# Two graph-attention layers: smaller gather batches, and a wait for a later tile's adjacency before each

## What is computed

```python
h = jnp.maximum(_layernorm(x, axis=-1), 0.0)
x = x + _L0_gnn_ref(h, adj, L0_gnn_W, L0_gnn_a)     # e = leaky_relu(s1_i + s2_j); softmax over adj > 0; elu(att @ hW)
h = jnp.maximum(_layernorm(x, axis=-1), 0.0)
x = x + _L1_gnn_ref(h, adj, Wq, bq, Wk, bk, Wv, bv) # e = q_i . k_j / sqrt(128);  softmax over adj > 0; elu(att @ v)
```

## Time and profile before

| | |
|---|---|
| median of 3 runs | 1950.41 us (1947.33 to 1957.92) |
| the profiled execution, its own time | 1946.39 us |
| its span, first to last instruction | 1944.6 us |
| start-up, first table of rows, first masks | to about 134 us, when the first gather goes out |
| first phase at its regular pace | about 152 to 925 us |
| its end without adjacency traffic | 925 to 1034 us |
| second phase | about 1056 to 1930 us |

### The profile page before, as it was taken

The page is one execution under the profiler, slowest core; times in us unless marked ns, Lnnn a source line. Parts: engine busy times, 40 slices in busy tenths (PEclk is TensorE's granted clock), DMA queues, the critical chain, the costliest instruction groups (busy, mean ns, idle before and its releaser), DMA issues.

```text
span 1944.6 us, 23228 instructions
## 1 busy us (share of the span) xinstructions
PE 1202.7 (62%) x5362; PEld 932.8 (48%) x5362; DVE 1290.0 (66%) x6912; ACT 766.3 (39%) x1507; POOL 1135.2 (58%) x1206
## 2 busy tenths in 40 slices
PE   2666767766677767766533456666565656556566
PEld 1444544443454445444433355555555555555555
DVE  4476888867898869877853455556565655556565
ACT  1966666656677758765111011111111111111111
POOL 1236666665666666665654566666666666666662
PEclk9887777777777777777555566666666666666665
DMA  9979999997999989995221112222222222222121
GB/s 307 408 283 398 389 367 350 359 330 274 368 393 388 326 315 387 384 370 180 56 53 45 44 49 55 53 54 54 49 55 53 55 54 55 54 54 54 48 56 35
DMA packets 122263, 372.41 MB, mean 192 GB/s; under 512 B 34577, under 2 KB 67858, under 8 KB 89362
## 3 DMA queue, kind: packets, MB, share of 16 engines
q1 hardware_dynamic: 75458, 289.83, 39.2%
q0 software_dynamic: 38464, 81.08, 15.5%
q10 hardware_dynamic: 8208, 0.03, 0.3%
HBM read 358.12 MB, written 12.72 MB: 191 GB/s over the span
## 4 chain that ended last, share of the span: by engine, by line
DVE 42%; another core or an unknown queue 21%; PE 13%; issue 9%; DMA 8%; ACT 3%; POOL 3%; SPq 1%; DVEq 0%; ACTq 0%; POOLq 0%
DVE arena L884 10%; DMA arena<-table,arena 6%; PE psum L1403 5%; DVE arena L1133 5%; POOL arena L580 3%; ACT arena L1184 2%; PE psum L1363 2%; DVE arena L877 2%; DMA table<-arena 2%; DVE arena L1137 2%; DVE arena L709 2%; DVE arena L902 2%; PE psum L1428 1%; DVE arena L768 1%
## 5 line engine op out<-in xcount | busy, mean ns | idle before, releaser
L580 POOL DMA_INDIRECT arena<-table,arena x576 | 555.8, 965 | 339.3 <-issue 204.7
L612 POOL DMA_INDIRECT arena<-table,arena x576 | 551.0, 957 | 327.2 <-DVE arena L893 159.5
L1184 ACT ACTIVATE arena<-arena 128x2048 bf16<-128x2048 int32 x256 | 485.7, 1898 | 58.0 <-remote 32.1
L1410 PE MATMUL psum<-arena 128*128 128x131 f32 (+1 forms) x768 | 193.1, 417 | 326.3 <-DVE arena L877 242.8
L1410 PEld LDWEIGHTS psum<-arena 128*128 128x128 f32 x768 | 160.4, 302 | 339.5 <-issue 336.4
L1363 PE MATMUL psum<-arena 128*128 128x512 bf16 x1024 | 309.4, 458 | 12.6 <-ACT arena L1184 12.6
L884 DVE SCALAR_TENSOR_TENSOR arena<-arena 128x131 f32<-128x131 f32 (+1 forms) x768 | 272.1, 354 | 18.8 <-DVE arena L884 2.2
L865 DVE TENSOR_TENSOR arena<-psum,arena 128x18 f32<-128x18 f32 x128 | 22.2, 174 | 326.9 <-remote 323.7
L1403 PE MATMUL psum<-arena 128*128 128x1 f32 x768 | 147.4, 307 | 148.0 <-DVE arena L867 137.3
L1403 PEld LDWEIGHTS psum<-arena 128*128 128x128 f32 x768 | 147.2, 273 | 181.3 <-DVE arena L867 158.5
L1320 ACT ACTIVATE arena<-psum 128x384 f32<-128x384 f32 x64 | 31.5, 492 | 425.8 <-remote 334.5
(11 more groups left out here) (199 smaller groups left out, 2112.9 us busy)
## 6 DMA issues: line engine op xcount, KB each, us to landing
arena<-in_adj_dram SPq DMA_DIRECT2D x256, 1024.0 KB
arena<-table,arena POOLq DMA_INDIRECT x1152
table<-arena POOLq DMA_DIRECT2D x32, 132.0 KB, 6.1
arena<-table SPq DMA_DIRECT2D x64, 66.0 KB
table<-arena SPq DMA_DIRECT2D x16, 256.0 KB
arena<-table SPq DMA_DIRECT2D x64, 64.0 KB
out_dram<-arena SPq DMA_DIRECT2D x16, 256.0 KB
arena<-in_x_dram SPq DMA_DIRECT2D x4, 0.5 KB, 12.2
```

The source lines that it names most:

```text
L580: pool.indirect_dma_start(Gt[:, v % GROUP, c + 1, :], None, table0, bass.IndirectOffsetOnAxis(idx_now[:, v % GROUP, c:c + 1], 0))\
L612: pool.indirect_dma_start(Gt[:, t % GROUP, c + 1, 0:D], None, table1, bass.IndirectOffsetOnAxis(idx_now[:, t % GROUP, c:c + 1], 0))\
L1184: nc.scalar.activation(mask[:, k, q * QUARTER:(q + 1) * QUARTER], adj_sb[:, k, q, :], ACT.Relu, accum_out=sum_all[:, bass.ds(tile, 1), q:q ...
L1410: last = nc.tensor.matmul(acc_ps[k][:, 0:width], weighted[:, c, :], Gt[:, r, OWN + c, 0:width], start=(c == 0), stop=(c == CHUNKS - 1))
```

## The change

The nine gathers of a tile are cut in four batches, of 3, 2, 2 and 2, in both phases. `landed` still asks for batch n-2, which now leaves at most five on the way (4, when both batches have two). In the first phase POOL waits in addition, ahead of batch b of tile v, for `mask_done` to reach 4(v+7)+b: for b = 0 that tile v+6 is masked entirely, for b = 1, 2, 3 that the first, the first two, the first three quarters of tile v+7 are masked. DVE waits for four semaphores of rows where it waited for three. The branch that isn't executed uses four semaphores of the second phase in place of its own `w_adj_used`.

```diff
@@ -34,8 +34,10 @@
 QCOLS = CHUNKS * 128
 GROUP = 4
 
-BATCH = 3
-BATCHES = 3
+FIRST = (0, 3, 5, 7, 9)
+BATCHES = 4
+SIZE = [FIRST[n + 1] - FIRST[n] for n in range(BATCHES)]
+BATCH_OF = [n for n in range(BATCHES) for _ in range(SIZE[n])]
 QUARTERS = 4
 WIDTH = 132
 LISTED = 129
@@ -366,7 +368,8 @@
         w_h_turned = sem("w_h_turned")
         w_ht_done = sem("w_ht_done")
         w_adj_in = [sem(f"w_adj_in{q}") for q in range(QUARTERS)]
-        w_adj_used = [sem(f"w_adj_used{q}") for q in range(QUARTERS)]
+
+        w_adj_used = [h_col_done, h_col_sb, u_done, u_kept]
         w_u_done = sem("w_u_done")
         w_ut_done = sem("w_ut_done")
         w_cbias_done = sem("w_cbias_done")
@@ -568,18 +571,21 @@
 
                 if n >= 0:
                     tile, nth = n // BATCHES, n % BATCHES
-                    pool.wait_ge(rows_in[tile % GROUP][nth], 16 * BATCH * (tile // GROUP + 1))
+                    pool.wait_ge(rows_in[tile % GROUP][nth], 16 * SIZE[nth] * (tile // GROUP + 1))
 
             for v in range(T):
                 if v >= GROUP:
                     pool.wait_ge(summed, v - 3)
                 pool.wait_ge(idx_done, v + 1)
                 for c in range(ROWS - 1):
-                    if c % BATCH == 0:
-                        landed(BATCHES * v + c // BATCH - 2)
+                    if c in FIRST:
+                        landed(BATCHES * v + BATCH_OF[c] - 2)
+
+                        if v + 7 < T:
+                            pool.wait_ge(mask_done, QUARTERS * (v + 7) + BATCH_OF[c])
                     pool.indirect_dma_start(Gt[:, v % GROUP, c + 1, :], None, table0,
                                             bass.IndirectOffsetOnAxis(idx_now[:, v % GROUP, c:c + 1], 0))\
-                        .then_inc(rows_in[v % GROUP][c // BATCH], 16)
+                        .then_inc(rows_in[v % GROUP][BATCH_OF[c]], 16)
 
             pool.wait_ge(flag_done, 1)
             whole = pool.value_load(flag[0:1, 0:1], min_val=0, max_val=1)
@@ -607,11 +613,11 @@
                     pool.wait_ge(summed, T + t - 3)
                     pool.wait_ge(idx_done, T + t + 1)
                     for c in range(ROWS - 1):
-                        if c % BATCH == 0:
-                            landed(BATCHES * (T + t) + c // BATCH - 2)
+                        if c in FIRST:
+                            landed(BATCHES * (T + t) + BATCH_OF[c] - 2)
                         pool.indirect_dma_start(Gt[:, t % GROUP, c + 1, 0:D], None, table1,
                                                 bass.IndirectOffsetOnAxis(idx_now[:, t % GROUP, c:c + 1], 0))\
-                            .then_inc(rows_in[t % GROUP][c // BATCH], 16)
+                            .then_inc(rows_in[t % GROUP][BATCH_OF[c]], 16)
 
 
         @block.vector
@@ -851,7 +857,7 @@
 
             def score0(u, k, r, n):
                 for batch in range(BATCHES):
-                    dve.wait_ge(rows_in[r][batch], 16 * BATCH * n)
+                    dve.wait_ge(rows_in[r][batch], 16 * SIZE[batch] * n)
                 dve.wait_ge(self_in[r], 16 * n)
                 nc.vector.tensor_tensor(e10[:, :], Gt[:, r, :, D], s1_10[:, r, :], ALU.add).then_inc(e_done, 1)
                 dve.wait_ge(e_done, u + 1)
@@ -1127,7 +1133,7 @@
 
                 def score1(u, b, k, n):
                     for batch in range(BATCHES):
-                        dve.wait_ge(rows_in[b][batch], 16 * BATCH * n)
+                        dve.wait_ge(rows_in[b][batch], 16 * SIZE[batch] * n)
                     dve.wait_ge(self_in[b], 16 * n)
                     for c in range(OWN):
                         nc.vector.scalar_tensor_tensor(out=prod[:, c, :], in0=Gt[:, b, c, 0:DE], scalar=SCALE, in1=u_row[:, b, P:],
```

## The result

The changed kernel takes 2055.41 us, the median of 4 runs (2045.34 to 2060.84), against 1951.41 us for the kernel before in the same measurement (4 runs, 1947.33 to 1957.92): a ratio of 1.0522, with a 95% interval of 1.0489 to 1.0556. It is 104 us slower; the forecast was 2035 us, 84 us slower. The profiled execution took 2054.3 us, its span is 2052.4 us, 107.8 us more than before.

What follows compares the result with a forecast made beforehand. First phase bound by transfers, its gather chain setting the pace up to 412 us; second phase not. 1946.4 + 85 (first phase; other terms 0) = 2031 us profiled, plus 4.0 to the median: 2035 us, range 1940 to 2085.

Steps and rivals of the forecast that it cites:

- The law of the chain: First phase, POOL's gathers: a tile costs 1.5L + 3.75 before, 2L + 3.75 after; 15.6 us a tile, +85 us.
- L: Time from the start of a batch's last gather to the start it releases; 6.65 us before by the law.
- The prediction's formula: First phase: L = 3.5 + 2.9 x 13.1/P for a tile of P us, giving P = 15.6.
- The unloaded end: L with DMA engines unloaded: taken as 3.5 us, between 2.9 and about 5.0.
- the loaded value: L with DMA engines loaded: taken as 6.4 us, range 6.2 to 6.65.
- the 6.54 us of tile 23's first batch: First phase after a 10 us pause: return time cited against the "faster" rival (L mostly queueing among gathers; 0.17, about 1922 us).
- The head start and the stall: First phase: the slower chain loses POOL's head start, swallows the 15.9 us ACT stall and stays late through tile 55.
- The mask wait at nothing: POOL's mask wait, first phase: free, as adjacency leads when gathers are late, and otherwise `score0` comes at least 13.8 us on.
- DVE's fourth wait at nothing: DVE's extra semaphore wait, ahead of L856 and L1133: under 2 us in each phase, taken as 0.
- bounds 0 and +10, taken as 0: Second phase: no wait if L is 3.5; at L of 5.0, 13.75 us of POOL against a 13.6 us period.
- The end of the first phase: 925 to 1034 us, without adjacency: POOL can send at 11.3 us a tile against 13.6 each; taken as 0.
- The rule weighed: Skill's DMA rule, about 2.0 us plus bytes: L an estimated 3.1, chain 10.0 us a tile, the change costing nothing.

Runs made afterwards that it cites:

- e1: Changed kernel without the mask wait (batches of 3, 2, 2, 2 in both phases): 2047.99 us, ratio 1.0472 to the kernel before.
- e5: Five batches of 2, 2, 2, 2 and 1, no mask wait: 2117.79 us, with 1989.43 for the kernel before on that chip.
- e13: Kernel before, its second phase pausing POOL ahead of the seventh gather until tile t-2's scatter matmuls are done; another chip: 1769.18 us, ratio 1.0001.
- e8: Batches of 3, 2, 2, 2 without mask wait, plus unused adjacency loads in the second phase: 2201.69 us, against 1952.28 before.
- e7: Kernel before (batches of three) plus unused adjacency loads, four quarters a tile, in the second phase: 1985.48 us, against 1952.28 before.
- e2: Kernel before, batches of three, plus only the mask wait: 1954.99 us, ratio 0.9996.
- e10: Kernel before with six of nine gathers a tile in the second phase, result incomplete: 1733.65 us, against 1952.28 before.
- e6: Changed kernel with each batch waiting for the landing of batch n-3 instead of n-2, both phases: 2007.18 us, ratio 1.0272.
- e12: Batches of 5 and 4 without mask wait (as another run), plus a POOL pause in each phase: 2003.91 us, ratio 1.0075 to the kernel before.

## Why the prediction was right

**The law of the chain held in the first phase.** Batches 0 and 2 of a tile form one chain, and it costs 2L + 3.75. Predicted 15.6 us a tile and 858 us for 55, measured 15.59 and 857.5. e1 has it without the mask, e5 with five batches, and e13 for three batches without any other limit. That the pace gives back a plausible L is no test by itself, since the distances on a chain add up to the pace whether POOL waits or not; the test is that POOL stood still before batch 2 in 54 of 56 tiles and before batch 0 in 41 of 55, and that `score0` waited behind them. One L for every batch was too simple: in e8 the other chain decides.

**L fell as it was made to.** The prediction's formula gives 3.5 + 2.9 x 13.1/15.6 = 5.94 us, and the measured pace 5.92. The unloaded end was a little low: in the new second phase, where adjacency is gone, released batches stand 3.8 to 4.3 us behind, not 3.5. With 4.0 in its place the formula would have said 15.7 us a tile. The DMA share came to 0.87 for 0.84. Only the reason for the loaded value had been argued; e7 shows it, by adding adjacency and nothing else. The argument itself had a hole: the 6.54 us of tile 23's first batch were not free of other gathers, for the three of the second batch went out while it was under way, between 456.84 and 463.38.

**The head start and the stall.** That the slower chain would swallow the single stall and stay late to tile 55 was right: `score0` waits 38 times, to the end. "Nearly every tile" was too much: it is 38 of 56, with 4.2 us a time (2 and more was said), and in the rest the rows were there first. POOL's landing waits number 109, or about 137 with those named after the mask but owed to landings, and I had said over 150: batches 1 and 3, on the chain with 1.25 us to spare, often find their landing there.

**The mask wait at nothing:** e2, 0.9996 (0.9959 to 1.0032). The prediction had two reasons, and both turned out to be needed: in the changed kernel the masks are ahead, and in e2, where they are not from tile 19 on, the wait is still free, since `score0` needs a batch only in a later iteration.

**DVE's fourth wait at nothing:** nothing in the profiles speaks against it; it was not tried by itself.

**What failed was the second phase, "bounds 0 and +10, taken as 0".** It measured +15.5 (+10 in e1). The working asked only whether POOL has the time, and L of 3.8 to 4.3 against a distance of 3.75 is a delay of a few tenths. I had not seen that the phase's period is tied to the end of POOL's run through DVE's wait (e10), so that there is no slack to take up a disturbance: in the pairs DVE meets a second wait of 4 us. What sets a pair off is open. The row that shows this wait, 303.4 us of 800, was in the trace of before and I had read only POOL's side of it. The end of the first phase, also 0, measured +4.7, and the start +3.0, neither of them traced to the change. These three and the smaller distance between profile and median (1.1 us here, 4.0 before) are the whole difference between 2035 and 2055.

**The rule weighed** ("DMA: Bandwidth & Descriptors", Anatomy of one DMA, SWDGE path, of the Trainium skill, about 2 us plus the bytes) would have had the change free. Under load no run comes near its estimate of 3.1 us: the released batches of after, e7 and e8 stand 5.6 to 8.3 us behind (medians by batch). The same page's section on latency expects a slower access under high load; e7 agrees in direction, with 6.9 to 7.7 us where at most 5.0 had been.

## What to carry to other kernels

Count, for each chain of batches that wait for landings, how many landings stand in it per tile: with a fixed lag of two batches, smaller batches put more landings in a row and cover each with less work, so the price in the first phase here was about half a landing a tile for the fourth batch. Price a landing from the busiest stretch in which it happens and not from a quiet one, and let the price fall with the DMA share that the new pace leaves. When a profile names a wait, compare its end with the end of what it names, and then ask whether anybody was waiting behind it: 67.6 us after were mostly not the masks', 66.2 us in e2 mostly were, and e2 is no slower for them. Do not take a rule that fits the total for shown until the places where it says an engine waits are found waiting (e8, e6). And before a wait is put in as a probe, work out that its value can be later than what has already been waited for.

## What the hardware showed that I had not expected

Gathers of the same size and order land in under 5.0 us alone and in 6.9 to 7.7 us when 1 MB quarters of adjacency flow (e7). In the changed kernel's second phase, where the next batch but one can start 3.75 us on, released batches stood 3.8 to 4.3 us behind.

On every chip but e13's, a wait of DVE in the second phase ended only when POOL's unbroken run of gathers did, about 2.7 us after its last start, while TensorE and ACT went on: 5.2 us in each of 58 tiles, and 3.5 us a tile less with three gathers fewer (e10). In e7 and e8, where POOL stops inside the run to wait for landings, such waits add up to 95 and 34 us in the whole kernel, against 396 before, and the wait of L865 is gone (L873 in e7, 1200 to 1900 us: no idle time listed). And in e12 DVE stood still 18 times where it waits for its own result alone. On e13's chip there was none in an unbroken run of any length, and the kernel before took 1768 us instead of 1952 or 1989. The Trainium skill ("SBUF — State Buffer", Who interferes with whom) has VectorE and GpSimd share a pair of ports, which one instruction can hold until it is done, but by the same section an instruction of VectorE with one input from SBUF, outside the 2-port modes, does not contend. L865 reads PSUM and SBUF, so by that it would not be held; and a wait of 5.2 us spans several gathers, with 0.3 us between one instruction of POOL and the next. No run here shows that it is the ports, and e13's chip, with the same instructions side by side and no wait, speaks against it as a rule. What holds DVE, and why not on every chip, stays open; e13's pause was not tried on a chip that has the wait.
